# Attention on one core: the products with V of two key blocks placed side by side, and a ring of eight instead of four exponentials

## The reference

```
x = x + 0.5 * moe_ffn(LN(x))     # 8 experts, top 2, F = 176, SiLU gate
x = x + attention(LN(x))         # 16 heads of 16, rotary, causal, S = 1024
x = x + 0.5 * moe_ffn(LN(x))     # the same weights again
```

```
scores = einsum('bhqd,bhkd->bhqk', q, k) / sqrt(16)   # + causal mask
probs  = softmax(scores)
ctx    = einsum('bhqk,bhkd->bhqd', probs, v)
```

## Time and profile before

| | us |
|---|---|
| median of three runs | 1250.35 (1248.92 to 1251.62) |
| the profiled execution | 1251.13 |
| its span, first to last instruction | 1249.4 |
| outside the span | 1.7 |
| attention, first to last product with V | 467.5 to 912.5 |
| PE busy over the span | 1011.6 (81%) |
| DVE busy over the span | 853.0 (68%) |
| ACT busy over the span | 643.0 (51%) |

### The profile page before, as it was taken

The page is one execution under the profiler, slowest core; times in us unless marked ns, Lnnn a source line. Parts: engine busy times, 40 slices in busy tenths (PEclk is TensorE's granted clock), DMA queues, the critical chain, the costliest instruction groups (busy, mean ns, idle before and its releaser), DMA issues. The chain is left out here.

```text
span 1249.4 us, 23740 instructions
## 1 busy us (share of the span) xinstructions
PE 1011.6 (81%) x6870; PEld 638.4 (51%) x6870; DVE 853.0 (68%) x2600; ACT 643.0 (51%) x1318; POOL 586.9 (47%) x756
## 2 busy tenths in 40 slices
PE   1647998973888389999999999999986559999850
PEld 1426997863777123333333333333265328988740
DVE  5684444434999498899899898989357674444437
ACT  1503555543777216676666666666764305555530
POOL 0936777774999302222222222222213907777750
PEclk9957999995999659999999999999988658999975
DMA  6802333334565511111111111110003503333349
GB/s 216 260 0 81 104 105 103 105 103 149 157 176 159 157 60 42 58 57 60 57 57 58 55 52 59 60 38 2 2 2 94 180 5 104 105 102 106 103 138 345
DMA packets 84523, 121.17 MB, mean 97 GB/s; under 512 B 10921, under 2 KB 63921, under 8 KB 81201
## 3 DMA queue, kind: packets, MB, share of 16 engines
q1 hardware_dynamic: 63424, 75.08, 18.9%
q0 software_dynamic: 13632, 37.24, 9.3%
q10 hardware_dynamic: 7344, 7.34, 1.7%
HBM read 75.51 MB, written 43.78 MB: 95 GB/s over the span
## 5 line engine op out<-in xcount | busy, mean ns | idle before, releaser
L1309 ACT ACTIVATE a_probs<-a_ps_s 128x1024 f32<-128x1024 f32 (+3 forms) x384 | 294.3, 813 | 175.2 <-PE a_ps_s L1341 174.0
L1224 POOL TENSOR_SCALAR_AFFINE_SELECT a_probs<-a_probs 128x256 f32<-128x256 f32 x256 | 102.5, 406 | 371.8 <-ACT a_probs L1309 369.1
L1242 DVE CUSTOM_DVE_ANT_0 a_unused<-a_ps_m,const_sb 128x128 bf16<-128x128 f32 (+3 forms) x512 | 234.2, 485 | 29.0 <-PE a_ps_m L1326 19.1
L1326 PE MATMUL a_ps_m<-st_k,st_q 96*128 96x512 bf16 (+3 forms) x768 | 220.5, 346 | 23.9 <-PEq L158 16.6
L1244 DVE TENSOR_REDUCE a_max_a<-a_ps_m 128x1 f32<-128x512 f32 x256 | 175.7, 686 | 14.1 <-PE a_ps_m L1326 13.9
L357 POOL DMA_INDIRECT v_sb<-xn_dram,f_token_i x142 | 137.6, 969 | 97.7 <-DVE f_token_i L468 55.0
L1341 PE MATMUL a_ps_s<-st_q,st_k 98*128 98x512 bf16 (+3 forms) x768 | 181.5, 330 | 1.5 <-ACT a_probs L1309 1.4
L1326 PEld LDWEIGHTS a_ps_m<-st_k,st_q 96*128 96x128 bf16 x768 | 68.1, 98 | 197.1 <-DVE a_max_a L1244 55.7
L492 DVE TENSOR_TENSOR f_h<-f_ps_gu,f_sg 128x176 f32<-128x176 f32 x142 | 48.4, 341 | 173.7 <-ACT f_sg L560 172.6
L1354 PE MATMUL a_ps_ctx<-a_probs,a_v_st 128*32 128x512 f32 (+3 forms) x1536 | 164.5, 500 | 1.3 <-POOL a_probs L1224 0.6
L361 POOL DMA_INDIRECT y_dram<-v_sb,f_pair_i x142 | 140.1, 987 | 43.3 <-issue 37.8
(11 more groups left out here) (183 smaller groups left out, 2013.9 us busy)
## 6 DMA issues: line engine op xcount, KB each, us to landing
xn_dram<-v_sb SPq DMA_DIRECT2D x64, 128.0 KB, 4.0
v_sb<-y_dram SPq DMA_DIRECT2D x32, 256.0 KB, 5.6
st_q<-qk_dram SPq DMA_DIRECT2D x16, 384.0 KB
st_k<-qk_dram SPq DMA_DIRECT2D x16, 384.0 KB
st_q<-y_dram SPq DMA_DIRECT2D x16, 256.0 KB, 3.1
st_k<-y_dram SPq DMA_DIRECT2D x16, 256.0 KB, 3.5
qk_dram<-st_rT_hi SPq DMA_DIRECT2D x16, 256.0 KB, 3.0
qk_dram<-st_rT_mid SPq DMA_DIRECT2D x16, 256.0 KB, 3.4
```

Of the source, the lines that this page charges most:

```text
L1224: pool.affine_select(out=tri, in_=tri, compare_op=ALU.is_ge, fill=zero, base=0, pattern=[[0, 2], [1, P]], channel_multiplier=-1).then_inc( ...
L1242: dve.tensor_tensor_reduce(unused[:, bank, 0:nk], ps, cst("mask")[:, HALF - nk:HALF], 1.0, NEG, ALU.add, ALU.max, at).then_inc(taken, 1)
L1309: act.activation(probs[:, s % 4, :, 0:nq], ps_s[s % 2][:, :, 0:nq], ACT.Exp, scale=float(HD) ** -0.5).then_inc(exp_done, 1)
L1326: pe.matmul(ps_m[bank][:, 0:nk], q_st[b][0:MAX_ROW, h, P * i:P * i + P], k_st[b][0:MAX_ROW, h, k0:k0 + nk], start=True, stop=True).then_in ...
```

## The change

Three things are changed, all in the attention.

1. The products with V come in pairs. Steps 5, 9, 13, 17 and 21 each issue two of them, directly one after the other: (0, 1), (2, 3), (4, 5), (6, 7), (8, 9). Step 1 issues products 10 and 11 of the group before. All other steps have none.
2. The ring of exponentials has eight places instead of four. The tile probs keeps four; the other four lie in the memory of the rT tiles, now one tile st_rT, which the projection has finished with. ACT therefore waits once, before its first exponential, until the projection's stores of those tiles have landed.
3. What hangs on the order moves: ctxT is copied out before the exponentials 3 and 11 instead of 2 and 10, it is turned in steps 6 and 14 instead of 5 and 12, and the planner is given the new places of the products, so that the first-pass units are spread anew.

```diff
-LAG = 3
+FIRST_V = 5
+PROBS = 8
...
+def products_after(s):
+    return [(s - FIRST_V) // 2, (s - FIRST_V) // 2 + 1] if s % 4 == FIRST_V % 4 else []
...
-    times = [nq + (V_SHARE * UNITS2[s - LAG][3] if s % 2 and s >= LAG else 0) for s, (_, _, _, nq, _) in enumerate(UNITS2)]
+    times = [nq + V_SHARE * sum(UNITS2[2 * v % N2][3] for v in products_after(s)) for s, (_, _, _, nq, _) in enumerate(UNITS2)]
...
-PASSED[LAG + 2].append(("sums", -1, 1))
-PASSED[12].append(("sums", 0, 0))
+PASSED[6].append(("sums", -1, 1))
+PASSED[14].append(("sums", 0, 0))
...
-        self.rT_hi, self.rT_mid, self.rT_lo = (
-            ctx.enter_context(nc.sbuf_tensor(f"st_rT_{part}", [P, RTS, 2 * KD, 2 * P], BF16)) for part in ("hi", "mid", "lo"))
+        rT = ctx.enter_context(nc.sbuf_tensor("st_rT", [P, 3, RTS, 2 * KD, 2 * P], BF16))
+        self.rT_hi, self.rT_mid, self.rT_lo = (rT[:, part, :, :, :] for part in range(3))
+        n = PROBS // 2 * 2 * HALF
+        self.probs_more = rT[:, :, :, :, :].rearrange("p z u c s -> p (z u c s)").bitcast(F32)[:, 0:n].rearrange("p (n h q) -> p n h q", h=2, q=HALF)
...
+    def wait_all_stored(self, act):
+        for u in range(RTS):
+            act.wait_ge(self.stored[u], 48 * len(range(u, NT // 2, RTS)))
...
-                    if s == 2 and not is_first(g):
+                    if s == 3 and not is_first(g):
                         evacuate(g - 1, 1, passed_before(g))
-                    if s == 10:
+                    if s == 11:
                         evacuate(g, 0, passed_before(g))
                     act.wait_ge(scored, N2 * g + s + 1)
-                    if not (is_first(g) and s < 4):
-                        act.wait_ge(pv_done, NV * g + s // 2 - 1)
+                    if not (is_first(g) and s < PROBS):
+                        act.wait_ge(pv_done, NV * g + s // 2 + 1 - PROBS // 2)
...
+            stacks.wait_all_stored(act)
             groups(act, group)
...
                     second_unit(g, b, s)
-                    if s == 1 and not is_first(g):
-                        times_v(g - 1, (b - 1) % RING, NV - 1)
                     pass_on(step[:SPLIT])
-                    if s % 2 == 1 and s >= LAG:
-                        if s == LAG:
-                            pe.wait_ge(v_copied, g + 1)
-                        times_v(g, b, (s - LAG) // 2)
+                    if s == FIRST_V:
+                        pe.wait_ge(v_copied, g + 1)
+                    for v in products_after(s):
+                        if v >= 0:
+                            times_v(g, b, v)
+                        elif not is_first(g):
+                            times_v(g - 1, (b - 1) % RING, NV + v)
                     pass_on(step[SPLIT:])
...
-            times_v(NGR - 1, (NGR - 1) % RING, NV - 1)
+            for v in (NV - 2, NV - 1):
+                times_v(NGR - 1, (NGR - 1) % RING, v)
             turn_ctx(NGR - 1, 1, TOTAL, TOTAL % 3)
```

More of the change, by code:

```diff
@@ L1126, in attention_phase, with probs @@
         v_st = [sb(f"v_st{i}", [P, TB, HG, 2 * HD]) for i in range(2)]
-        probs = sb("probs", [P, 4, 2, HALF])
+        probs_own = sb("probs", [P, PROBS // 2, 2, HALF])
+        def probs(n):
+            return probs_own[:, n % PROBS, :, :] if n % PROBS < PROBS // 2 else stacks.probs_more[:, n % PROBS - PROBS // 2, :, :]
         unused = sb("unused", [P, 3, HALF], BF16)
@@ L1222, in group @@
                     pool.wait_ge(exp_done, N2 * g + n + 1)
-                    tri = probs[:, n % 4, :, 0:P]
+                    tri = probs(n)[:, :, 0:P]
                     pool.affine_select(out=tri, in_=tri, compare_op=ALU.is_ge, fill=zero, base=0, pattern=[[0, 2], [1, P]],
@@ L1301, in group @@
                 for s, (half, j, q0, nq, pair) in enumerate(UNITS2):
-                    if s == 2 and not is_first(g):
+                    if s == 3 and not is_first(g):
                         evacuate(g - 1, 1, passed_before(g))
-                    if s == 10:
+                    if s == 11:
                         evacuate(g, 0, passed_before(g))
                     act.wait_ge(scored, N2 * g + s + 1)
-                    if not (is_first(g) and s < 4):
-                        act.wait_ge(pv_done, NV * g + s // 2 - 1)
-                    act.activation(probs[:, s % 4, :, 0:nq], ps_s[s % 2][:, :, 0:nq], ACT.Exp, scale=float(HD) ** -0.5).then_inc(exp_done, 1)
+                    if not (is_first(g) and s < PROBS):
+                        act.wait_ge(pv_done, NV * g + s // 2 + 1 - PROBS // 2)
+                    act.activation(probs(s)[:, :, 0:nq], ps_s[s % 2][:, :, 0:nq], ACT.Exp, scale=float(HD) ** -0.5).then_inc(exp_done, 1)
+            stacks.wait_all_stored(act)
             groups(act, group)
@@ L1354, in times_v @@
                     mm = pe.matmul(ps_ctx[32 * h:32 * h + 32, q0 - HALF * half:HALF], v_st[b % 2][:, j, h, :],
-                                   probs[:, (2 * v + h // 2) % 4, h % 2, 0:nq], start=(j == 0), stop=(j == 4 * half + 3),
+                                   probs(2 * v + h // 2)[:, h % 2, 0:nq], start=(j == 0), stop=(j == 4 * half + 3),
                                    skip_group_check=True)
```

## The result

| | before | after |
|---|---|---|
| median of the runs, us | 1249.9 (1248.92 to 1251.62, 4 runs) | 1316.26 (1313.45 to 1319.02, 4 runs) |
| ratio to before, 95% interval | | 1.0529 [1.0503, 1.0555] |
| span of the profiled execution, us | 1249.4 | 1313.7 |
| first to last product with V, us | 445.0 | 505.2 |

The change makes the kernel 5.3% slower; forecast were 1312 us and a range from 1268 to 1338. Of the 64.3 us between the two spans, 60.2 lie between the first product (471.5) and the last (976.7). The other 4 lie ahead of it. The first product stands in step 5 instead of 3, and the attention's first matmul comes 1.8 us later (431.5 instead of 429.7). This second part need not be the change's: over the kernels of the experiments that matmul lies anywhere from 428.9 to 431.6.

A forecast was written before the change was run, and what follows sets the result against it. PE looks like the bound, but pairs leave DVE and ACT without work: 4.1 us more a group over about 15 groups, 1251.1 + 62 = 1313, median 1312 us; own range 1278 to 1338, stated range 1268 to 1338.

The forecast's parts named there:

- The bound: Steady attention: PE looks like the bound at 29.8 of 30 us, but about 1.5 us of a 28.46 us group are waits.
- The saving: Each pair enters and leaves the products once, not twice: 6 x 0.24 = 1.44 us a group, 23 us in 16 groups.
- The prediction's sign of 1.9 to 2.0 from the start: Sign of being right: pairs of 512s take 1.9 to 2.0 us from start to the next matmul.
- the two bounds: Saving per pair: nothing if the second product pays its own passage, 0.24 us if it follows at once; 0.24 taken.
- The walk: New order followed with trace durations, pair end to pair end: 32.6 us a group instead of 28.5, +4.1.
- The edges: Last group: 1 to 3 us added for scores held back by exponentials; as much taken off for the first group.
- What was to cost nothing: Ring of eight places, ACT's wait for the projection's stores, POOL's cut and SP's order: no added time expected.
- just in time: DMA of the maxima lands in 3.2 us before the next group's scores; if late, up to 0.7 us a group.
- The whole saving: Rival: the 0.24 us saved 96 times comes through whole, 1250 - 23 = 1227 us; chance 7%.
- About equal: Rival: the planner's order around the pairs makes up most of the gap, 20 to 35 us lost, 1248 to 1262; 6%.
- A lower clock: Rival: granted clock falls in part of PE's standing; for a tenth of the attention +45 us, 1360 and more; 3%.
- Products that do not stand together: Rival: V1 of a pair waits for an exponential or a cut, about 1270 us; 2%.

The follow-up runs named there:

- DVE shortened: DVE reads only 128 columns of every first-pass unit, output differs: changed kernel 1282.73 us, kernel before 1233.53 us.
- both readers shortened: DVE reads 128 columns of each first-pass unit, ACT exponentiates 128 of each score unit, output differs: changed kernel 1230.59 us, kernel before 1225.99 us.
- an order made from the waits: Changed kernel with ctxT copies back before exponentials 2 and 10 and the planner's step weights set: 1261.84 us, 1.0101.
- The short pairs: Single products, early copies, hand-set weights, only products 2, 3 and 10, 11 joined: 1239.03 us, again 1239.75; same weights with every product alone 1242.04.

## Why the prediction was right

- **The bound.** That PE shown as busy was not simply the bound held: with DVE shortened, a group of the kernel before became 0.98 us shorter, and the changed kernel as it is has PE less busy and a longer time.
- **The saving.** One passage of 0.24 us less for each pair: the pair of 512s takes 1.86 us from its start and 1.95 with the 0.09 on entering it, as forecast. (The prediction's sign of 1.9 to 2.0 from the start is missed by 0.04, because this way lies ahead of the start.) Of the two bounds, the one taken was right. Its weights go in while the first product streams (645.08).
- **The walk.** Pair end to pair end, forecast and measured: steps 13 to 17 7.4 and 7.41; 17 to 21 5.7 and 5.68; 21 to 1 3.8 and 3.82; 1 to 5 4.9 and 4.89; 5 to 9 4.7 and 4.70; 9 to 13 6.0 and 6.01. A group 32.6 and 32.51; the stretches as they are printed in the prediction add up to 32.5. The waits stand where the walk had them: the fourth unit at 647.66, and the scores for exponentials in steps 5 (behind the copy), 13 (643.82), 20 and 21 (656.63 and 657.33).
- **The edges.** The last group, from its first scores to its last product, takes 25.4 us (951.10 to 976.52) instead of 23.0 (889.38 to 912.35), within the 1 to 3 us allowed. Not counted were the 4 us ahead of the first product, part of them perhaps scatter. Between first and last product 60.2 us came instead of the 62. The two together make 64.3; the rest of the difference between 1312 and 1316 lies within the spread of the runs (1313.45 to 1319.02).
- **What was to cost nothing.** Ring, new memory and ACT's wait: shown by the run of single products with early copies. The list of waits names none for the maxima's DMA, but "just in time" was right: with both readers shortened, scores wait for it 4.8 us in 350.
- **What it did not say.** The prediction told of DVE's standing first and of ACT's waits second. Taken out in this order, ACT's two buffers carry the larger part. The sum did not depend on it, because the walk had both.
- **Some luck.** The forecast set the walk's 32.6 us against the measured 28.46. The same walk of the order before, done later, gives 28.0 and not 28.46; had the change been the difference of two walks, it would have been 4.6 us a group and about 1319. That too lies within the range, so the range did not need the luck; the 4 us between 1312 and 1316 did.
- **The rivals.** The whole saving: refuted, and not only by starvation, since it does not show even with short readings. About equal: the planner's order around the pairs did not make up the gap; an order made from the waits does so to 1%. A lower clock: 1.00 from 490 to 960. Products that do not stand together: all sixteen records of a pair are one group in the timeline.

The Trainium skill (TensorEngine Tiling (Array Packing), PSUM Bottleneck) says that tiling speeds up TensorE but not the emptying of PSUM. No run here sets tiled products beside untiled ones, so none tests that sentence. What the traces show is another case: the banks that ran empty are those of other matmuls, ps_m and ps_s, and their readers were not too slow in the mean (DVE 23.3 and ACT 17.8 of 30 us); what they had in their banks did not last for the 1.95 us. Whether more banks would do is not shown, since no run has more.

Left open: the same walk gives 28.0 us for the order before, where 28.27 to 28.46 are measured, and is short by 0.3 to 0.5 us for the other orders, except where long pairs lie as the planner puts them (32.6 and 32.51, 31.5 and 31.53). What these 0.3 to 0.5 us are was not looked for.

## What to carry to other kernels

Before putting work of one kind together, take the time of the longest block and compare it with what the other engines hold in their buffers at that moment: here 1.95 us of PE against three banks of at most 0.61 us and two exponentials of 0.93. A saved 0.24 us is lost several times over when two readers run dry, and with engines that execute in order, whatever stands behind the waiting instruction is lost too. The short pairs, 0.88 us each by the same sum, gained 2.3 us. In such a pipeline the order of filler work is the cheaper lever: weights set from the waits gave 8 us without any pair, and 39 us back with them. And walk one period with durations from the trace: it foretold each stretch of the changed kernel to some 0.03 us, and the group of other orders to 0.5.

## What the runs showed that was not expected

With both readers shortened, so that a reading lasts 0.29 us and an exponential 0.38, PE's 25.5 us of columns and passages in the order with pairs still take 27.61 us a group. The prediction did not have this; the walk done for that run gave 27.2. By that walk it is the ways between the engines, 0.21 us from PE's last column to a reader's start and about 0.05 to 0.06 back, that with three and two banks take more than the six saved passages give. No run shortens the ways, so this is argued and not shown, and 0.4 us of the 27.61 stay open.
